# A recurrence that runs as two chains from its first step, with row pieces of 256 elements, inside a fused recurrent and gated block on one core

## What is computed

```python
x = L0_attn_x                                   # (2, 1024, 512)
# 1: u = layernorm(x) @ W_in.T + b_in           (hidden 1024)
#    s_t = tanh(u_t + s_(t-1) * gamma + beta)   over the 1024 positions, one after another
#    y = s @ W_out.T + b_out
#    x = x + layernorm(y)
# 2: h = layernorm(x)
#    z = ((silu(h @ q(gate_w) * gate_scale) * (h @ q(up_w) * up_scale)) @ q(down_w)) * down_scale
#    x = x + layernorm(z)                        (inner 1536)
# q() rounds a weight to float8_e4m3fn and back to float32
```

## Time and profile before

| | |
|---|---|
| median of 3 runs | 580.43 us |
| lowest and highest | 580.22, 582.93 us |
| the profiled execution | 580.79 us |
| its span, first to last instruction | 579.0 us |
| PE, DVE, ACT, POOL busy in the span | 553.5, 447.2, 371.6, 204.5 us |

### The profile page before, as it was taken

How to read it: one execution, slowest core, us unless ns; L and a number is a source line. 1 busy time by engine, 2 the same in 40 slices (tenths; PEclk the granted TensorE clock), 3 DMA queues, 4 the chain that set the end, 5 groups by cost and what they waited for, 6 DMA issues and landing times.

```text
span 579.0 us, 11854 instructions
## 1 busy us (share of the span) xinstructions
PE 553.5 (96%) x2984; PEld 462.6 (80%) x2984; DVE 447.2 (77%) x2607; ACT 371.6 (64%) x2284; POOL 204.5 (35%) x339
## 2 busy tenths in 40 slices
PE   8999899899988999999999999999999999999993
PEld 5767667889776988788988799778986897889992
DVE  3689899996796888888988887789868988754313
ACT  3687687855686767866777677767776776523330
POOL 1214316435252323533334333152214341732622
PEclk9999999999998999999999999999999999999997
DMA  7878369800102001010102010020000200200000
GB/s 253 285 225 244 60 201 208 170 0 2 38 1 74 1 2 38 31 45 1 38 2 73 2 38 1 1 74 2 2 1 2 73 2 2 72 1 2 1 36 37
DMA packets 20069, 33.89 MB, mean 59 GB/s; under 512 B 2720, under 2 KB 4896, under 8 KB 20000
## 3 DMA queue, kind: packets, MB, share of 16 engines
q1 hardware_dynamic: 16544, 26.84, 13.8%
q0 software_dynamic: 3456, 6.29, 6.1%
HBM read 22.63 MB, written 4.19 MB: 46 GB/s over the span
## 4 chain that ended last, share of the span: by engine, by line
DVE 50%; ACT 24%; PE 17%; issue 5%; POOL 2%; SPq 0%; DMA 0%; POOLq 0%; DVEq 0%; ACTq 0%
DVE recur L1160 14%; ACT pairs L1466 10%; PE gate_up L1067 8%; DVE recur L1169 6%; DVE recur_second L1160 6%; DVE fused L1297 5%; ACT pairs L1450 4%; PE wide L1090 4%; ACT fused_hi L1509 3%; DVE peaks L1362 3%; ACT gated L1493 3%; PE wide L1026 3%; DVE powers L1345 2%; ACT pairs L1470 2%; DVE rounders L1352 2%
## 5 line engine op out<-in xcount | busy, mean ns | idle before, releaser
L1466 ACT ACTIVATE pairs<-recur 128x8 f32<-128x8 f32 x768 | 138.4, 180 | 100.2 <-DVE recur L1160 99.6
L1160 DVE TENSOR_TENSOR_SCAN recur<-recur,pairs 128x16 f32<-128x16 f32 x768 | 151.3, 197 | 56.0 <-ACT pairs L1466 51.8
L1592 POOL TENSOR_TENSOR fused_lo<-fused,fused_hi 128x256 fp32r<-128x256 f32 x96 | 71.1, 741 | 200.2 <-ACT fused_hi L1509 200.2
L1466 ACT ACTIVATE pairs<-recur_second 128x8 f32<-128x8 f32 x768 | 138.3, 180 | 0.0
L1160 DVE TENSOR_TENSOR_SCAN recur_second<-recur_second,pairs 128x16 f32<-128x16 f32 x768 | 133.4, 174 | 0.0
L1026 PE MATMUL wide<-w_out_sb,pairs 128*128 128x512 f32 x256 | 117.3, 608 | 5.7 <-ACT pairs L1466 5.7
L1067 PE MATMUL gate_up<-x_hi,gate_q 128*128 128x256 f32 x384 | 103.3, 302 | 3.5 <-DVE fused L1297 2.4
L1026 PEld LDWEIGHTS wide<-w_out_sb,pairs 128*128 128x128 f32 x256 | 74.4, 298 | 38.5 <-ACT pairs L1466 7.5
L1004 PE MATMUL wide<-x_norm_t,w_in_sb 128*128 128x256 f32 x448 | 101.0, 380 | 2.3 <-DVE y L1208 2.2
L1004 PEld LDWEIGHTS wide<-x_norm_t,w_in_sb 128*128 128x128 f32 x448 | 84.5, 190 | 16.0 <-issue 3.1
L1067 PE MATMUL gate_up<-x_lo,up_q 128*128 128x256 f32 x384 | 95.9, 283 | 0.0
(11 more groups left out here) (126 smaller groups left out, 763.8 us busy)
## 6 DMA issues: line engine op xcount, KB each, us to landing
x_in<-x SPq DMA_DIRECT2D x16, 256.0 KB, 3.3
x_res<-x SPq DMA_DIRECT2D x16, 256.0 KB, 3.2
out<-z SPq DMA_DIRECT2D x14, 256.0 KB, 2.5
w_in_sb<-w_in_t SPq DMA_DIRECT2D x4, 512.0 KB, 6.1
w_out_sb<-w_out_t SPq DMA_DIRECT2D x8, 256.0 KB, 4.3
raw_own<-down_w SPq DMA_DIRECT2D x8, 256.0 KB, 3.8
raw_own<-rounders POOLq DMA_DIRECT2D x6, 256.0 KB, 4.5
raw_own<-gate_w SPq DMA_DIRECT2D x5, 256.0 KB, 4.1
```

The source lines that it names most:

```text
L1160: eng.tensor_tensor_scan(preact_of[b].rearrange("p c k -> p (c k)"), factors_of[b].rearrange("p c k -> p (c k)"), pairs[:, (t - 1) % RING, ...
L1466: eng.activation(pairs[:, t % RING, columns, 0], preact_of[b][:, :, 1], ACT.Tanh).then_inc(s_state_of[b], 1)
L1592: eng.tensor_tensor(fused_lo[:, f, :], fused[:, f, :], fused_hi[:, f, :].bitcast(F32), ALU.subtract).then_inc(s_fused_lo, 1)
```

## The change

- The recurrence runs as two chains from step 0. Each chain has a PSUM bank of its own (`recur0`, `recur1`), which leaves two banks instead of three for the rounding on PE. The step that prepared the second chain goes.
- Every LayerNorm piece has 256 elements, and `fused` is never cut: one instruction of 256 tokens for each chunk. `row_parts` and `chunk_parts` go.
- The planner stretches PE, POOL and queue lengths by 1.05 from step 0 on, the search for the weights' largest values may begin at step 120 instead of 60 (`PEAKS_FROM`), and in block 0's part of PE's order the transposes of block 1's x1 stand elsewhere.
- `BETWEEN` has y in other places: parts of tile 0 are spread over several places, and y of the very last tile (block 7, tile 1) stands ahead of chunk 5 of block 6 instead of chunk 4.

```diff
-TWO_CHAINS_FROM = 2
-def row_parts(kind, n, b, last):
-    if kind == "x":
-        return 4 if n >= TWO_CHAINS_FROM + 2 else 2
-    if kind in ("z", "low"):
-        return 2
-    return 2 if n < 2 or (n, b) == (last, 1) else 4
-def chunk_parts(p, last):
-    return 2 if 1 <= p < last else 1
...
-                if engine not in ("vector", "scalar") and self.two_chains_from <= now < self.last_step:
+                if engine not in ("vector", "scalar") and 0 <= now < self.last_step:
                     steps *= PACE
...
 BETWEEN = {
-    4: {3: "y101", 4: "y123", 6: "x0 x1", 7: "u0", 8: "u1", 9: "u2", 10: "u3", 14: "Y001", 15: "Y023 t0 t1 Y1"},
-    5: {12: "t0", 13: "t1", 14: "Y001", 15: "Y023"},
-    6: {4: "y1", 12: "t0 t1"},
+    4: {1: "y03", 3: "y101", 4: "y123", 6: "x0 x1", 7: "u0", 8: "u1", 9: "u2", 10: "u3", 14: "Y001", 15: "Y02 t0 t1 Y03"},
+    5: {1: "y101", 2: "y123", 12: "t0", 13: "t1", 14: "Y00", 15: "Y01"},
+    6: {1: "y02", 2: "y03", 5: "y1", 12: "t0 t1"},
 }
-PEAKS_FROM = 60.0
+PEAKS_FROM = 120.0
...
-        for m in range(1, KH // 2):
-            if m == 2:
-                split_next(1, [0])
-            project_u(3, m, rank(n, 4))
+        project_u(3, 1, rank(n, 4))
+        split_next(1, [0])
+        project_u(3, 2, rank(n, 4))
         split_next(1, [1])
+        project_u(3, 3, rank(n, 4))
         project_y(2, 0, rank(n, 6), [0, 1])
...
-        round_banks = [recur_second[:, :], wide[2][:, :], wide[3][:, :]]
+        round_banks = [wide[2 + b][:, :] for b in range(batch)]
...
-                    eng.tensor_tensor_scan(preact.rearrange("p c k -> p (c k)"), factors.rearrange("p c k -> p (c k)"),
-                                           pairs[:, (t - 1) % RING, :, :].rearrange("p c k -> p (c k)"), 0.0,
-                                           ALU.mult, ALU.add).then_inc(s_preact, 1)
+                    for b in range(batch):
...
+                        eng.tensor_tensor_scan(preact[b].rearrange("p c k -> p (c k)"),
+                                               factors[b].rearrange("p c k -> p (c k)"),
+                                               pairs[:, (t - 1) % RING, b * KH:(b + 1) * KH, :].rearrange(
+                                                   "p c k -> p (c k)"), 0.0, ALU.mult, ALU.add).then_inc(s_preact[b], 1)
```

More of the change, by code:

```diff
@@ L237, in transpose_x @@
     def transpose_x(n, b, k):
-        after = [(v, 0.2) for v in rows("y", "y_copy", n - 2, b)] if n >= 4 else []
+        after = [(v, 0.2) for v in pair("y_copy", n - 2, b)] if n >= 4 else []
         if n == 3:
-            after = [(v, 0.2) for v in tokens("fuse", 0, KI - NG + b)]
+            after = [(("fuse", 0, KI - NG + b), 0.2)]
         t.tensor(("t1", n, b), TRANSPOSE_STEPS, [(("x_norm", n, b), 0.2)] + after, k)
@@ L438, in lay_first @@
         next_x(n + 1)
-        low = [(v, 0.2) for b in range(batch) for v in rows("low", "x1_low", p, b)]
+        low = [(v, 0.2) for b in range(batch) for v in pair("x1_low", p, b)]
         for i in range(KI):
@@ L490, in timetable @@
                 if i < KI:
-                    low = [(v, 0.2) for b in range(batch) for v in rows("low", "x1_low", p, b)] if i == 0 else []
+                    low = [(v, 0.2) for b in range(batch) for v in pair("x1_low", p, b)] if i == 0 else []
                     gate_up(p, i, low, rank(n - 1, 4.5) + 0.01 * i)
@@ L500, in timetable @@
     for i in range(KI):
-        low = [(v, 0.2) for b in range(batch) for v in rows("low", "x1_low", LAST, b)] if i == 0 else []
+        low = [((*("x1_low", LAST, b), h), 0.2) for b in range(batch) for h in range(2)] if i == 0 else []
         gate_up(LAST, i, low, rank(LAST, 4.5) + 0.01 * i)
@@ L508, in timetable @@
         norm_z(LAST, b, ("down", LAST, KI - 1), rank(NB, 10 + b))
-    last_piece = max(i for i in range(NP) if not by_transfer(i))
-    for h in range(2):
-        side("vector", ("second", h), [(v, 0.2) for v in pair("take", last_piece)], 90.0)
     t.jobs["down", 0, KI - 1].after.append((("guard", 3), 0.2))
@@ L1241, in measure_x1 @@
                 for n in range(NB):
-                    for h in row_pieces("r", n, b):
+                    for h in range(2):
                         yield at["r_half", n, b, h]
@@ L1268, in low_x1 @@
                 for n in range(NB):
[L1269 to L1270 removed]
+                    for h in range(2):
                         yield at["x1_low", n, b, h]
[L1272 removed]
+                        ks = slice(h * KD // 2, (h + 1) * KD // 2)
                         if h == 0:
```

297 lines of the change are left out of this document (111 added, 186 removed), and 6 rows, old and new, of the table BETWEEN.

## The result

| | before | after |
|---|---|---|
| median | 580.4 us | 595.92 us (594.26 to 596.67) |
| the profiled execution, its span | 580.79, 579.0 us | 596.67, 594.5 us |
| first scan | 17.8 us | 18.1 us |
| first 256 steps | 127.7 us | 128.2 us |
| steps 256 to 1023 | 356.1 us | 369.0 us |

The ratio of the mean times is 1.0254, with an interval of 1.0216 to 1.0291. By the medians the changed kernel is slower by 15.5 us. Of the 15.5 us between the two spans, 12.9 us lie in steps 256 to 1023. The profiled execution is the slowest of the four of the changed kernel, 0.75 us above the median.

The account below looks back on a forecast made before the run. The prediction took the chain's steps, set by what stands between their scans, as the bound, with PE balanced against it at the end. +10.5 + 0.5 + 1.1 = +12.1 us on 580.4 gave 592.5 us, range 584 to 599.

Parts of the forecast that it names:

- The prices of the steps: Two-chain step lengths by the DVE piece between scans: free 0.444 us, `fused` on 256 tokens 0.57, `powers` 0.52, constant 0.51.
- Part 1: Steps 256 to 1023: larger DVE pieces between the scans lengthen steps, +10.5 us (8 to 14).
- I take 1.9 us off for such stalls: Steps 256 to 1023: longer steps give PE 3% more time, so fewer stalls from late PE, 1.9 us off (0 to 3).
- the term for gates that fall together with a large piece: Steps 256 to 1023: where ACT's gate meets a large DVE piece only the longer counts, 1.5 us off (0 to 3).
- rival D: At each y PE waits longer, its clock falls to 1.2 GHz, the chain stalls four times: 7 us more, 599.5 us; chance 0.08.
- A: The forecast itself: what stands between the scans sets the step; likeliest 592.5 us, 588 to 598, chance 0.74.
- Part 2: First 256 steps as two chains: the shorter way's gain is eaten by large pieces, +0.5 us (-2 to +4).
- an allowance for stalls: First 256 steps: 3.3 us added for stalls and dearer pieces, since ACT's slots cost something with two chains.
- Part 3: Behind the chain: last y waits for gate, `fused` and chunk 4, with one chunk less after it, +1.1 us (-0.5 to +2.5).
- Rival B: Whole kernel: PE is the real bound, so its unchanged work keeps the time, 581 us; chance 0.12.
- Rival C: Whole kernel: DVE's total time counts, so fewer, larger pieces make it faster, 572.6 us; chance 0.06.

Follow-up runs that it names:

- the changed kernel (filled): Changed kernel with 17 and 22 unread products in PE's waits for the low part of x1 in blocks 2 and 4: 593.63 us.
- the kernel before (filled): Kernel before with 24 unread products on PE ahead of y of block 2, tile 0, where it waited for the tanh: 579.65 us.
- The single edit: Kernel before with two chains from step 0, two rounding banks and the search for largest values from step 120; small pieces and places of y kept: 585.50 us.

## Why the prediction was right, and where its sum was short

The time, 595.9 us, is 3.4 us above the 592.5 us forecast and inside the range; the sign, and the stretch from which the loss comes, were right.

**The prices of the steps** held (medians of the trace). `fused` on 256 tokens: 0.564 us (0.55 to 0.58 forecast); a free step: 0.442 us (0.44); the copy of z 0.50 us, the low part of x1 0.50 us, statistics 0.49 us, normalisations 0.49 us; `powers` 0.52 us on average and the constant 0.51 us, which the prediction had only bounded.

**Part 1**, +10.5 us forecast, +12.9 us measured. The term that was mis-sized is the last one, "I take 1.9 us off for such stalls". The runs let it be split. Without falls of the clock in this stretch, the changed kernel (filled) takes 365.8 us and the kernel before (filled) 354.5 us: the larger pieces cost 11.3 us, where 13.9 - 1.5 = 12.4 us were forecast. With the measured prices the counts still make about 13.8 us, so the term for gates that fall together with a large piece, 1.5 us, would have to be about 2.5 us; no run takes it apart. The falls of the clock cost 3.2 us in the changed kernel (369.0 less 365.8) and 1.6 us before (356.1 less 354.5): instead of 1.9 us less they are 1.6 us more. 11.3 + 1.6 = 12.9 us. The prediction reasoned that longer steps give PE more time, so that it would be late less often. This is so, and it is just what makes it wait: PE's few waits for the tanh went from 5.7 to 0.4 us, and those for the low part of x1 rose from 1.0 to 6.3 us, with the clock at 1.2 GHz behind two of them. That is rival D's mechanism, in two places instead of four, at other waits than the ones it named, and on top of A rather than in its place. These are single executions, and another one of the same order had only the first of the two falls (366.5 us).

**Part 2**, +0.5 us forecast, +0.5 us in the changed kernel's trace (128.2 against 127.7 us). That it is exact is luck: 3.3 us of the sum were an allowance for stalls, and an early fall of the clock, which some executions have, moves the stretch by 1.3 to 1.9 us. The single edit showed 130.1 us in an execution with an early fall of the clock, within the upper bound of +4 us.

**Part 3**, +1.1 us forecast, +1.8 us measured. The y starts 5.0 us after the chain's end, where 4.1 us (3.8 + 0.3) were forecast, but for another reason. I had PE waiting for `fused` of chunk 2. It does not wait: it still has most of chunk 3, then chunk 4 to do, since the planner's order puts the whole of PE's work later in steps. The right sign of this part is luck: the wait that it was worked out from is not there. The later plan alone (two chains from step 0, old place of y) costs 2.4 us behind the chain, and moving the y from chunk 4 to chunk 5 costs nothing. The first scan came 0.3 us later in the profiled execution, which makes the miss of the three parts and the first scan: 2.4 + 0.0 + 0.7 + 0.3 = 3.4 us.

**Rival B** (PE's work bounds the time, 581 us) is excluded: PE's products are the same and the time is not. **Rival C** (DVE's sum counts) too: DVE's busy time fell by 17.2 us and the time rose. The Trainium skill, "VectorE: DVE Perf Modes", section "The TRN2 errata — SBUF-src ops pay a fixed extra latency per instruction", says that one large tile pays the fixed latency once and many small ones pay it each. DVE's sum agrees, 430.0 against 447.2 us, but the kernel's time does not follow that sum.

**Do the parts add?** Alone against before, the medians rose by 6.0 us (`fused`), 4.1 us (LayerNorm pieces) and 4.4 us (two chains from step 0), 14.5 us of the 15.5 us. That is partly chance: the first two together cost 13.5 us, so the two chains and the new places, on top of these, cost only about 2 us. The changed kernel with the old places has large pieces and two chains and lies 12.6 us above the kernel before, so on top of the large pieces the two chains cost nothing that a median shows, and the 2 us would be the new places'; but the intervals of these ratios overlap. That the transposes of block 1's x1 stand elsewhere was not tried alone, and `PEAKS_FROM` only together with the two chains.

## What to carry to other kernels

Where a fixed chain of short instructions shares an engine with other work, cut that work so that a piece fits into the idle time of one step: the larger piece has less overhead, and every step in which it stands is longer (0.444 us with 128 tokens of `fused`, 0.564 us with 256). A change of the step's length also shifts every engine against the fixed order: list the waits of the engine that gets ahead, and look whether its clock falls behind them and who is queued behind it then. If it falls, products that nobody reads, about as long as the wait, can win time (1.6 us in one place, 3.2 us in two), but look at each trace again, since another wait may then cost it. And take more than one trace: the same wait in the same program had a fall behind it in one execution and none in another.

## What the runs showed of the hardware

**The same wait does not always cost the clock.** Early in the program, ahead of a projection to u, PE waits 2.16 us for the copy of y. In the profiled execution of the kernel before, the clock stayed at 1.00; in that of the kernel with the filled wait at 173 us, whose instructions are the same up to there, it fell. PE and DVE, before:

```profile
61.05 7.14 PE L1004 MATMUL wide<-x_norm_t,w_in_sb 128*128 128x256 f32 x32 [2.16 <-DVE y L1208]
```

```profile
65.30 0.23 DVE L1169 TENSOR_TENSOR_SCAN recur<-recur,pairs 128x32 f32<-128x32 f32 x1 [1.04 <-ACT pairs L1470]
```

and with the filled wait:

```profile
61.19 8.83 PE L1005 MATMUL wide<-x_norm_t,w_in_sb 128*128 128x256 f32 x32 [2.17 <-DVE y L1215]
```

```profile
67.13 0.23 DVE L1176 TENSOR_TENSOR_SCAN recur<-recur,pairs 128x32 f32<-128x32 f32 x1 [2.72 <-ACT pairs L1477]
```

32 products take 1.7 us longer, and the scan waits 1.7 us longer. Of the six profiled kernels that share this part, step 93 lasts 1.57 us in three and 3.24 to 3.25 us in the three with the fall, after waits of 2.16 to 2.18 us in all. The executions of the kernel before lie in two groups, near 580.7 and near 582.6 us. The granted clock, averaged over an execution, is 0.990 to 0.992 in all those beside the experiments that took up to 581.4 us, and 0.986 to 0.989 in all that took 581.56 us or more. A fall like that behind the wait of 3.9 us, 3.4 us at half the clock, lowers that average by 0.003 (an estimate from the trace), so the slower ones have about one fall more; where it lies in each, the record does not show. The Trainium skill, "TensorE: Matmul & The Clock Gate", section "What's actually happening", says that the gate's monitor runs free of the kernel and that the number of slow products at a kernel's start differs from run to run. These rows show such a difference in the middle of a program.

**Unread products kept the clock up.** 22 or 24 products of 128x256, 3.2 and 3.1 us of work in the middle of waits, kept the granted clock at 1.00 in these places. They promise nothing for the next wait: with old places and products together the clock fell at 496.6 us, behind a wait of 1.92 us.
